# Layer 4 cross-attention: head results kept transposed and moved by DMA, inverses in small rows, the running maxima turned in fp32r

## The reference, cut to what matters

```python
q = split_heads(query @ Wq.T + bq)          # B=4, 16 heads, 256 tokens, 16 channels
k = split_heads(key @ Wk.T + bk)            # 4096 context tokens
v = split_heads(value @ Wv.T + bv)
scores = jnp.einsum('bhqd,bhkd->bhqk', q, k) / np.sqrt(HEAD_DIM)
weights = jax.nn.softmax(scores, axis=-1)
out = jnp.einsum('bhqk,bhkd->bhqd', weights, v)
out = out.transpose(0, 2, 1, 3).reshape(b, -1, D_MODEL)
return out @ Wo.T + bo
```

## Time and profile before

| | us |
|---|---|
| median of 3 runs | 2063.71 (2060.92 to 2065.98) |
| profiled execution, its own time | 2062.04 |
| its span, first to last instruction | 2060.7 |
| PE, DVE, ACT, POOL busy | 1822.7, 1514.8, 1215.3, 236.1 |
| mean granted TensorE clock | 0.942 |

### The profile page before, as it was taken

How to read it: one execution, slowest core, us unless ns; L and a number is a source line. 1 busy time by engine, 2 the same in 40 slices (tenths; PEclk the granted TensorE clock), 3 DMA queues, 4 the chain that set the end, 5 groups by cost and what they waited for, 6 DMA issues and landing times. The chain is left out here.

```text
span 2060.7 us, 33466 instructions
## 1 busy us (share of the span) xinstructions
PE 1822.7 (88%) x12885; PEld 1243.7 (60%) x12885; DVE 1514.8 (74%) x1789; ACT 1215.3 (59%) x2167; POOL 236.1 (11%) x270
## 2 busy tenths in 40 slices
PE   7989998878888885899998899999999999998754
PEld 5877785456655553678887455555555555555524
DVE  6546543379988995565655789998988998993574
ACT  1333332577667753353433188888888888884463
POOL 4223301000000000232221000010010000000000
PEclk8999998999999997999999599999999999999986
DMA  9798842257755752121204846556644845500000
GB/s 362 262 334 314 321 144 88 72 179 259 248 193 207 249 207 70 62 67 65 87 30 82 170 84 111 112 98 107 124 89 88 147 84 109 101 23 6 0 0 21
DMA packets 164206, 276.99 MB, mean 134 GB/s; under 512 B 16833, under 2 KB 92865, under 8 KB 156881
## 3 DMA queue, kind: packets, MB, share of 16 engines
q1 hardware_dynamic: 162320, 274.36, 47.5%
q10 hardware_dynamic: 1728, 0.49, 0.1%
HBM read 186.45 MB, written 88.08 MB: 133 GB/s over the span
## 5 line engine op out<-in xcount | busy, mean ns | idle before, releaser
L2171 DVE TENSOR_REDUCE xn_peaks<-psum 128x2 f32<-128x1024 f32 x512 | 623.2, 1225 | 69.4 <-PE psum L1995 65.4
L2131 ACT ACTIVATE moe_mix_transposed<-psum 128x512 f32<-128x512 f32 x1024 | 552.2, 597 | 67.8 <-PE psum L2000 18.4
L2000 PE MATMUL psum<-xn_q_stack,xn_k_words 50*128 50x256 f32 x2048 | 379.0, 308 | 6.8 <-DVE xn_peaks L2171 3.1
L1995 PE MATMUL psum<-xn_k_words,xn_q_stack 50*128 50x512 f32 x1024 | 377.0, 458 | 6.1 <-DMA xn_q_stack<-q_rows 3.3
L2000 PEld LDWEIGHTS psum<-xn_q_stack,xn_k_words 50*128 50x128 f32 x2048 | 251.1, 187 | 202.5 <-ACT moe_mix_transposed L2131 174.6
L2032 PE MATMUL psum<-moe_mix_transposed,xn_v 128*32 128x256 f32 x4096 | 328.8, 393 | 1.9 <-issue 0.3
L1995 PEld LDWEIGHTS psum<-xn_k_words,xn_q_stack 50*128 50x128 f32 x1024 | 187.2, 188 | 16.5 <-issue 11.6
L1133 DVE TENSOR_TENSOR_SCAN mx_state<-mx_decay,mx_state 128x1024 f32<-128x1024 f32 x64 | 151.5, 2366 | 4.2 <-POOL mx_decay L858 4.2
L321 PE MATMUL psum<-xw_ctx_natural,xw_weights_transposed 128*128 128x256 f32 x512 | 126.3, 393 | 13.4 <-DVE xw_weights_transposed L473 13.2
L2032 PEld LDWEIGHTS psum<-moe_mix_transposed,xn_v 128*32 128x32 f32 x4096 | 81.7, 108 | 73.5 <-issue 7.6
L723 ACT ACTIVATE ctx_k_words<-psum,ctx_bk 128x512 fp32r<-128x512 f32 x128 | 86.4, 683 | 57.3 <-PE psum L153 35.4
(11 more groups left out here) (321 smaller groups left out, 2639.5 us busy)
## 6 DMA issues: line engine op xcount, KB each, us to landing
xn_k_words<-k_words SPq DMA_DIRECT2D x384, 128.0 KB, 6.7
ctx_words<-xw_ctx_transposed_words SPq DMA_DIRECT2D x64, 512.0 KB, 7.0
ctx_chunk_words<-ctx_words SPq DMA_DIRECT2D x64, 512.0 KB, 5.3
k_words<-ctx_k_words SPq DMA_DIRECT2D x128, 256.0 KB, 2.3
v_all<-ctx_v SPq DMA_DIRECT2D x32, 544.0 KB, 3.1
xn_v<-v_all SPq DMA_DIRECT2D x32, 544.0 KB, 4.8
...
```

The costliest lines, as they stand in the source:

```text
L1995: return pe.matmul(PS[:, 2 * (x % 2) + a, :], Q[narrow_rows(a), m // XN_PAIRS % 2, m % XN_PAIRS, q * P:(q + 1) * P], K[m % XN_KSLOTS][narr ...
L2000: return pe.matmul(PS[:, narrow_bank("exp", n, step, a), half * S:(half + 1) * S], K[n % XN_KSLOTS][narrow_rows(a), kt * P:(kt + 1) * P], ...
L2131: act.activation(t["weights"][:, step % 4, a, :, :], bank.rearrange("p (t s) -> p t s", t=2), ACT.Exp, scale=XN_SCALE).then_inc(s.taken, 1)
L2171: dve.tensor_reduce(t["peaks"][:, m % 2, q, :, c], PS[:, 2 * (x % 2):2 * (x % 2) + 2, :], AX.X, ALU.max).then_inc(s.top_read, 1)
```

## The change

The turned results go. `sums` becomes two tiles in alternation. A new SP function, `head_rows`, copies each quarter's 16 rows of sums by DMA straight to the rows of their channels in `O`, which now is transposed (channels along the partitions, the two halves of the context side by side), and each denominator row of 256 numbers to eight rows of 32 in `den`: eight DMAs for each unit, issued behind the unit's twelve key loads. After the last unit of a batch DVE (`inverted`) adds the two halves of the denominators and takes one reciprocal for all heads, behind the maxima of step 8 of the next batch's first unit. SP (`spread_inverses`) writes them to HBM and reads them back broadcast to 16 rows a head. POOL adds the two halves of `O` (`halves`), DVE multiplies by the inverses (`normalised`, second unit, step 1), PE projects (second unit, before step 5), and DVE adds to x (second unit, step 8). The transposes of `O` and the copies behind them are gone.

The maxima are turned by two fp32r matmuls of 128 x 128 words (a padded `neg_words` against an fp32r identity) where there were four fp32 ones, eight with second passes, of two columns of weights. POOL clears the padding once at the start, and ACT makes the fp32r identity.

The core of the diff:

```diff
-    if step == 3 and n:
-        uses.append(("turned", n - 1))
...
-    if n and n % XN_PAIRS == 0:
-        if step == 10:
-            uses.append(("out", n // XN_PAIRS - 1))
-        if step == 12:
-            uses.append(("projected", n // XN_PAIRS - 1))
+    if n > XN_PAIRS and n % XN_PAIRS == 1 and step == 5:
+        uses.append(("projected", n // XN_PAIRS - 1))
     if step == 14 and n + 1 < XN_N:
         uses.append(("shift", n + 1))
...
-XN_LAST = [("turned", XN_N - 1), ("out", B - 1), ("projected", B - 1)]
+XN_LAST = [("projected", B - 1)]
...
+
+    def head_rows(n):
+
+        b, pair = n // XN_PAIRS, n % XN_PAIRS
+        sp.wait_ge(s.acc, n + 1)
+        if n:
+            sp.wait_ge(s.o_in, 64 * n)
+            sp.wait_ge(s.den_in, 64 * n)
+        if b and pair == 0:
+            sp.wait_ge(s.o, b)
+        for a in range(2):
+            head = 2 * pair + a
+            c, first = head * XN_DH // P, head * XN_DH % P
+            for half in range(2):
+                at = XN_W * (2 * half + a)
+                sp.dma_start(t["O"][first:first + XN_DH, c, half, :], t["sums"][at:at + XN_DH, n % 2, :]
+                             ).then_inc(s.o_in, 16)
+                sp.dma_start(t["den"][head * XN_SPREAD:(head + 1) * XN_SPREAD, half, :],
+                             t["sums"][at + XN_DH:at + XN_VW, n % 2, :].rearrange("o (e s) -> o e s", e=XN_SPREAD)
+                             ).then_inc(s.den_in, 16)
+
+    def spread_inverses(b):
+
+        sp.wait_ge(s.den, 2 * (b + 1))
+        sp.dma_start(Rd[b].rearrange("h (e s) -> (h e) s", e=XN_SPREAD), t["den"][:, 0, :]).then_inc(s.r_out, 16)
+        sp.wait_ge(s.r_out, 16 * (b + 1))
+        for c in range(KD):
+            heads = Rd[b, c * P // XN_DH:(c + 1) * P // XN_DH]
+            sp.dma_start(t["rsum"][:, c, :], heads[:, None, :].to_broadcast([P // XN_DH, XN_DH, S])).then_inc(s.r_in, 16)
...
+        head_rows(n)
+        if n % XN_PAIRS == XN_PAIRS - 1:
+            spread_inverses(n // XN_PAIRS)
...
+    def halves(b):
+
+        pool.wait_ge(s.o_in, 64 * XN_PAIRS * (b + 1))
+        if b:
+            pool.wait_ge(s.made, XN_USE["projected", b - 1] + 1)
+        pool.tensor_tensor(t["OT"], t["O"][:, :, 0, :], t["O"][:, :, 1, :], ALU.add).then_inc(s.halves, 1)
...
+    pool.tensor_copy(t["neg_words"][:].rearrange("p q a r -> p (q a r)"), k.zero[:, 0:1].to_broadcast([P, QT * P])
+                     ).then_inc(s.pads, 1)
...
     def shift_rows(m):
         free("shift", m)
         pe.wait_ge(s.words, 2 * (m + 1))
-        for a in range(2):
-            for q in range(QT):
-                last = pe.matmul(PS[narrow_rows(a, XN_SHIFT, XN_LOW), narrow_bank("shift", m), q * P:(q + 1) * P],
-                                 t["neg_words"][:, q * 2 + a, :].bitcast(F32), k.ident[:], start=True, stop=True)
-        last.then_inc(s.made, 1)
...
-    def turned(n):
-        free("turned", n)
-        pe.wait_ge(s.acc, n + 1)
         for q in range(QT):
-            last = pe.matmul(PS[:, narrow_bank("turned", n), q * XN_HALF:(q + 1) * XN_HALF],
-                             t["sums"][:, q * P:(q + 1) * P], t["sel"][:], start=True, stop=True)
...
+            last = pe.matmul(PS[:, narrow_bank("shift", m), q * P:(q + 1) * P],
+                             t["neg_words"][:, q, :, :].rearrange("p a r -> p (a r)"), t["ident"][:], start=True, stop=True)
         last.then_inc(s.made, 1)
 
     def projected(b):
         free("projected", b)
-        pe.wait_ge(s.taken, XN_USE["out", b] + 1)
+        pe.wait_ge(s.o, b + 1)
...
     def accumulated(n):
         act.wait_ge(s.sum, XN_STEPS * (n + 1))
-        if n:
-            act.wait_ge(s.made, XN_USE["turned", n - 1] + 1)
-        act.copy(t["sums"][:], PS[:, XN_ACC, 0:S]).then_inc(s.acc, 1)
+        if n >= 2:
+            act.wait_ge(s.o_in, 64 * (n - 1))
+            act.wait_ge(s.den_in, 64 * (n - 1))
+        act.copy(t["sums"][:, n % 2, :], PS[:, XN_ACC, 0:S]).then_inc(s.acc, 1)
...
-    def reciprocal_sum(n):
-        dve.wait_ge(s.taken, XN_USE["turned", n] + 1)
-        if n:
-            dve.wait_ge(s.o, n)
-        dve.reciprocal(t["rsum"][:], t["turned"][:, :, :, XN_DH]).then_inc(s.rsum, 1)
+    def inverted(b):
+
+        dve.wait_ge(s.den_in, 64 * XN_PAIRS * (b + 1))
+        dve.tensor_tensor(t["den"][:, 0, :], t["den"][:, 0, :], t["den"][:, 1, :], ALU.add).then_inc(s.den, 1)
+        dve.wait_ge(s.den, 2 * b + 1)
+        dve.reciprocal(t["den"][:, 0, :], t["den"][:, 0, :]).then_inc(s.den, 1)
+
+    def normalised(b):
+        dve.wait_ge(s.r_in, 32 * (b + 1))
+        dve.wait_ge(s.halves, b + 1)
+        dve.tensor_tensor(t["OT"], t["OT"], t["rsum"][:], ALU.mult).then_inc(s.o, 1)
...
-        if n > 0 and step == 6:
-            reciprocal_sum(n - 1)
-        if n > 0 and n % XN_PAIRS == 0 and step == 15:
+        if n > 0 and n % XN_PAIRS == 0 and step == 8:
+            inverted(n // XN_PAIRS - 1)
+        if n > XN_PAIRS and n % XN_PAIRS == 1 and step == 1:
+            normalised(n // XN_PAIRS - 1)
+        if n > XN_PAIRS and n % XN_PAIRS == 1 and step == 8:
             projected(n // XN_PAIRS - 1)
...
-    reciprocal_sum(XN_N - 2)
     ffn_weight_dve(k, 2)
-    reciprocal_sum(XN_N - 1)
+    inverted(B - 1)
+    normalised(B - 1)
```

More of the change, by code:

```diff
@@ L1730, in narrow_tiles @@
          "peaks": sb("peaks", [P, 2, QT, 2, CH]),
-         "neg": sb("neg_max", [P, 2, QT * 2]), "neg_words": sb("neg_words", [P, QT * 2, 2], F32R),
-         "sel": sb("sum_of_halves", [P, XN_HALF]), "sums": sb("sums", [P, S]), "turned": sb("turned", [P, QT, 2, XN_W]), "rsum": sb("rsum", [P, QT, 2]),
-         }
+         "neg": sb("neg_max", [P, 2, QT * 2]), "neg_words": sb("neg_words", [P, QT, 2, XN_HALF], F32R),
+         "ident": sb("identity_words", [P, P], F32R), "sums": sb("sums", [P, 2, S]),
+         "den": sb("denominators", [P, 2, S // XN_SPREAD]), "rsum": sb("rsum_by_channels", [P, KD, S])}
     late = k.moe_mixT[:].rearrange("p e s -> p (e s)")
     t["weights"] = late[:, 0:16 * S].rearrange("p (i a t s) -> p i a t s", i=4, a=2, t=2)
-    t["O"] = late[:, 16 * S:20 * S].rearrange("p (i q d) -> p i q d", i=2, q=QT)
+    t["O"] = late[:, 16 * S:20 * S].rearrange("p (c i s) -> p c i s", c=KD, i=2)
     t["OT"] = late[:, 20 * S:22 * S].rearrange("p (c s) -> p c s", c=KD)
@@ L1743, in narrow_sems @@
 def narrow_sems(k):
-    s = k.sems("xn", "mix_pe mix_r mixed stats aggr root rstd y wq k_ones weights pads zeros made taken qlo q_out q_in top top_read neg words sum acc rsum sel o wide row plus x")
+    s = k.sems("xn", "mix_pe mix_r mixed stats aggr root rstd y wq k_ones weights pads zeros made taken qlo q_out q_in top top_read "
+                     "neg words sum acc o_in den_in r_out r_in halves den ident o wide row plus x")
     return s, [k.xn_keys_in] + [k.sem_row(f"xn_keys{slot}_", XN_KHALVES) for slot in range(1, XN_KSLOTS)], k.sem_row("xn_values", 2)
@@ L1838, in words @@
             pool.wait_ge(s.made, XN_USE["shift", m - 1] + 1)
[L1839 removed]
+        neg = t["neg"][:, m % 2, :].rearrange("p (q a) -> p q a", a=2)
+        pool.tensor_copy(t["neg_words"][:, :, :, XN_SHIFT], neg).then_inc(s.words, 1)
         pool.wait_ge(s.words, 2 * m + 1)
[L1841 removed]
+        pool.tensor_tensor(t["neg_words"][:, :, :, XN_SHIFT + 1], neg, t["neg_words"][:, :, :, XN_SHIFT].bitcast(F32),
                            ALU.subtract).then_inc(s.words, 1)
[L1844 to L1851 removed]
+    def halves(b):
[3 more added lines that the diff above has]
+        pool.tensor_tensor(t["OT"], t["O"][:, :, 0, :], t["O"][:, :, 1, :], ALU.add).then_inc(s.halves, 1)
     pool.memset(t["V"][:, :, XN_KT * 2 * XN_VW:], 0.0).then_inc(s.pads, 1)
     pool.wait_ge(s.pads, 1)
+    pool.tensor_copy(t["neg_words"][:].rearrange("p q a r -> p (q a r)"), k.zero[:, 0:1].to_broadcast([P, QT * P])
+                     ).then_inc(s.pads, 1)
+    pool.wait_ge(s.pads, 2)
     zeros(0)
@@ L1870, in narrow_pool @@
             zeros(n // XN_PAIRS + 1)
-        if n:
-            normalised(n - 1)
+        if n and n % XN_PAIRS == 0:
+            halves(n // XN_PAIRS - 1)
         if n == 0:
@@ L1881, in narrow_pool @@
             pool.tensor_tensor(k.X[:, n - 1, :], k.X[:, n - 1, :], t["row"][:], ALU.add).then_inc(s.plus, 1)
-    normalised(XN_N - 1)
+    halves(B - 1)
 def narrow_pe(k, t, sems):
@@ L1973, in projected @@
         last.then_inc(s.made, 1)
-    between = {"normed": normed, "query": query, "row": row_constant, "shift": shift_rows, "turned": turned, "out": transposed_out,
-               "projected": projected}
+    between = {"normed": normed, "query": query, "row": row_constant, "shift": shift_rows, "projected": projected}
     def maxima_ready(x):
@@ L2106, in shift_rows @@
         last.then_inc(s.taken, 1)
-    def turned(n):
-        bank = made("turned", n)
-        if n:
-            act.wait_ge(s.o, n)
-        act.copy(t["turned"][:].rearrange("p q h n -> p (q h n)"), bank[:, 0:QT * XN_HALF]).then_inc(s.taken, 1)
```

(7 more changed lines are left out.)

27 lines of the change are left out of this document (3 added, 24 removed).

## The result

| | before | after |
|---|---|---|
| median of 4 runs, us | 2064.85 (2060.92 to 2066.36) | 2097.8 (2093.14 to 2107.33) |
| ratio of the runs | | 1.0168, 95% interval [1.0142, 1.0194] |
| profiled execution, us | 2062.04 | 2107.33 |
| PE, DVE, ACT, POOL busy, us | 1822.7, 1514.8, 1215.3, 236.1 | 1838.0, 1520.7, 1207.0, 234.6 |
| mean granted clock | 0.942 | 0.918 |

The account below looks back on a forecast made before the run. PE was taken to bound the kernel. From the profiled 2062.04 us, -18.0 (sums), -5.8 (maxima), +47.7 (batch ends) and +10.1 (end of the loop) gave +34.0, so 2096 us, range 2064 to 2112.

Parts of the forecast that it names:

- PE is the pace: In the loop, PE sets the pace, DVE 8% behind; ordinary units were to become shorter by 0.8 us.
- Turnings of the sums, -18.0: In the loop, 31 turnings of the sums on PE go, at 0.58 us each: -18.0 us.
- Turnings of the maxima, -5.8: In the loop, 31 turnings of the maxima take 0.25 us instead of 0.44 on PE: -5.8 us.
- The denominators come late: At three batch ends, denominators land behind the keys at about 1366.0; PE stands 4.6 us before step 11.
- the upper bound of 6: Upper bound for one PE gap at a batch end, with 1.5 us more of writing in small pieces.
- The clock falls with the gap and full-width matmuls bring it back: At three batch ends, the clock halves as the gap ends and stays until the projection: 11.9 us each.
- The rival of the short spell: At batch ends the gap comes, but the clock returns after one short spell: 2069 us, chance 0.14.
- The sum: Whole kernel: sums -18.0, maxima -5.8, batch ends +47.7, end of the loop +10.1, together +34.0 us.
- The end, +10.1: Behind the loop's last unit, the projection starts later, after the denominators' DMAs, at half clock: +10.1 us.
- The rival "in time" at 2047: At batch ends, denominators land before 1362, so no gap and no clock fall: 2047 us, chance 0.13.

Follow-up runs that it names:

- E5: Changed kernel with head-row DMAs ahead of the key loads, and multiplication by inverses, projection and addition to x later: 2048.32 us; again 2051.21 us.
- E4: Kernel before, with only the maxima turned by two fp32r matmuls as in the changed kernel: 2063.39 us, ratio 0.998 to before.
- E1: Changed kernel with each unit's eight head-row DMAs issued ahead of its twelve key loads: 2071.49 us, ratio 1.0013 to before.
- E2: Changed kernel with DMAs unmoved, but the denominators' sum and reciprocal, multiplication, projection and addition to x placed later: 2073.09 us, ratio 1.0037 to before.
- E7: E5 plus eight unread DVE reductions behind (8, 7), (16, 7) and (24, 7), far from the projection: 2082.26 us, ratio 1.0069 to before.
- E6: E5 with the four denominator DMAs issued ahead of the four of the sums: 2055.77 us; again 2053.77 us.
- E9: E5 plus eight unread DVE reductions behind (9, 5), (17, 5) and (25, 5), near the projection: 2080.97 us, ratio 1.0072 to before.
- E12: A further run that the text given neither describes nor gives a time for.
- E3: Changed kernel plus four unneeded full-width fp32 matmuls before (8, 12), (16, 12) and (24, 12), behind each gap: 2088.27 us, ratio 1.01 to before.
- E10: E6 with the row constant's full-width matmuls of unit 0 before step 1, not step 6: 2046.77 us, ratio 0.9913 to before.
- E8: E5 plus eight unread DVE reductions behind (9, 7), (17, 7) and (25, 7), the projection falling into the gap: 2070.7 us, ratio 1.0022 to before.

## Why the prediction was right

**PE is the pace.** Right. Units without a batch end became 0.68 us shorter (20.96 to 20.28 from one turning of the maxima to the next), 0.77 was forecast; DVE's groups stayed at 1225 ns and its idle time in the loop rose. E5's loop, with nothing but less work on PE, is 22.9 shorter.

**Turnings of the sums, -18.0.** Right. With the transposes (3 x 0.59 = 1.8) and the maxima (2) they make 21.8 of E5's 22.9 (22.4 without the start).

**Turnings of the maxima, -5.8.** Mis-sized: -2. The pair takes 0.44 on the timeline, its first-to-next pitch 0.38, where the pitch of a long row of fp32r matmuls gave 0.25. Two matmuls with full weight loads between other work aren't a row of 31. E4 bounds it within noise, the traces give 0.06 each.

**The denominators come late.** Right in place and chain (E1, E2 and E5 each take the wait away and most of the loss goes), mis-sized in time. The issues take 0.53 to 0.66 each and not 0.45, 5.1 for eight where 3.6 was forecast, and the packets land 17.0, 14.2 and 15.7 us behind the sums and not 13.9. What differs between the batches is the queue: the last key load landed at 1363.9, 1548.3 and 1733.5, and DVE was released 1.7, 1.3 and 1.2 us behind that. Gaps 8.60 + 4.85 + 6.37 = 19.8 us; 13.8 was forecast, and the upper bound of 6 for one was passed twice. The price of issuing the denominators' pieces was taken from the queries' rows, which turned out cheaper.

**The clock falls with the gap and full-width matmuls bring it back.** The fall is right, three times of three, but it came 6.8, 2.0 and 2.9 us ahead of the gaps' ends, not as they ended. The price forecast was 3 x 11.9 = 35.7; after's loop is 48.0 over E5's, of which 19.8 are gaps, so 28.2. A spell costs only while PE runs: that was 66.8 of its 78.5 us, where the forecast had counted with some 26 a spell, 79 in all. At 2.165 us a step for 1.235 the 66.8 are worth 66.8 x 0.43 = 28.7 (an estimate), close to the 28.2.

What ends a spell was read too strictly from rows 10 and 11 ("it did not rise in these steps"). In the first two batches the clock was low until the projection; in the third it was back at 1754.1 with the projection at 1756.79, and so, ahead of the projection, in E2 and E7. At the start of the loop too it was back ahead of the row constant in six of the thirteen traces that have it before step 6, in after (1187.52 and 1187.53) and E6 by 0.2 us or less, in E1, E4, E9 and E12 by some 2.6. What holds is weaker: inside the loop no spell outlasted such matmuls by more than 0.9 us (E1, E3, E9, E10, after twice), and in plain steps it ended after anything from 3.4 (E8) to 27.3 us (E7). At the end of the loop, where PE stands ahead of the projection and again behind it, the spell outlasted the projection by more than that in seven traces of fourteen: in E5 the clock was half from 1844.6 to 1868.5, with the projection from 1855.97 to 1859.73. The rival of the short spell is thus not excluded by mechanism but by how seldom it came, and was rightly left with a chance.

**The sum.** Gaps 6.0 too short, clock 7.5 too dear, maxima 3.8 too good: these offset each other but for 2. The chain is shown, but that the total came within 1 us of the difference of the medians is luck in part.

**The end, +10.1.** +10.8. The eight issues took 5.0 us from 1894.05 and not 3.6, but the last landed within 1.1 of its issue's end and not 2.2; the way to the projection was 0.9 longer in all, the projection 0.25 shorter.

**What the prediction had not seen**: two more waits turn up when the first is mended. The inverses' way behind the keys (E1) is a wait only when the denominators are early, since in after the keys have landed before the write is issued. `halves` ahead of the words in POOL's queue (E2) costs nothing in after, because PE stands then anyway. The rival "in time" at 2047 therefore needed more than a landing before 1362: E1, which had it, came out at 2071, and E5, with the second wait gone too, at 2048 to 2051.
